# GPS layer, edge loop: edge attributes staged per batch of 28 items by one gather and one store, in place of per round of 56 items by two

## The reference

```
s     = leaky_relu(x_l[src] + x_r[dst] + e_attr @ W_e.T, 0.2)   # 4 heads of 64
alpha = einsum('ehc,hc->eh', s, att)
alpha = softmax of alpha over the edges of one dst
out   = segment_sum(alpha[..., None] * x_l[src], dst)
```

## Time and profile before

| | |
|---|---|
| median of 3 runs | 3459.81 us (3458.88 to 3461.9) |
| span of the profiled execution | 3452.9 us |
| edge loop within it | about 116 to 1530 us |
| PE, DVE, ACT, POOL busy in the whole span | 88%, 53%, 44%, 34% |

### The profile page before, as it was taken

One profiled execution on the slowest core, in us unless ns is written; L12 is line 12 of the kernel. 1 busy time (PEld: TensorE's weight loads), 2 busy tenths in 40 slices (PEclk: granted clock), 3 DMA queues, 4 the chain that ended last, 5 costly groups with the idle time before them and its releaser, 6 DMA issues. The chain is left out here.

```text
span 3452.9 us, 50836 instructions
## 1 busy us (share of the span) xinstructions
PE 3048.3 (88%) x13612; PEld 2420.6 (70%) x13613; DVE 1834.2 (53%) x3643; ACT 1508.7 (44%) x4936; POOL 1189.9 (34%) x1152
## 2 busy tenths in 40 slices
PE   6678888788888888884999999999999999999999
PEld 5456656566565665563778877877787888888898
DVE  5566666666676666676754564374365435111103
ACT  2067666777667676775322322232231212222232
POOL 4556555565555655630310031030021001222210
PEclk9899899999999999997999999999999988999999
DMA  7556655555665655554211011100001032333361
GB/s 217 152 148 148 145 145 141 143 144 141 149 145 145 147 142 150 136 94 124 52 38 37 27 30 31 41 8 1 15 27 50 1 100 84 128 120 119 119 176 38
DMA packets 288628, 345.06 MB, mean 100 GB/s; under 512 B 155176, under 2 KB 213655, under 8 KB 284512
## 3 DMA queue, kind: packets, MB, share of 16 engines
q1 hardware_dynamic: 232813, 174.79, 19.1%
q0 software_dynamic: 53632, 157.89, 17.6%
q10 hardware_dynamic: 2064, 10.81, 1.0%
HBM read 298.03 MB, written 44.37 MB: 99 GB/s over the span
## 5 line engine op out<-in xcount | busy, mean ns | idle before, releaser
L1470 POOL DMA_INDIRECT a_g<-xl_d,a_ix x480 | 468.1, 975 | 311.6 <-issue 116.0
L1504 PE MATMUL b_pM<-b_m,b_oh 128*112 128x281 f32 x1680 | 513.6, 451 | 28.5 <-DVE g_acc L1644 22.5
L1599 ACT ACTIVATE b_m<-a_g,c_pcx 128x64 f32<-128x64 f32 x1856 | 460.4, 334 | 33.6 <-issue 33.6
L1504 PEld LDWEIGHTS b_pM<-b_m,b_oh 128*112 128x112 f32 x1680 | 327.6, 200 | 156.7 <-issue 69.0
L1470 POOL DMA_INDIRECT XS<-xl_d,a_ix x344 | 333.3, 969 | 216.5 <-issue 91.1
L1637 DVE SCALAR_TENSOR_TENSOR a_r<-a_pS,g_attx 128x528 f32<-128x528 f32 x420 | 286.6, 699 | 198.4 <-remote 91.6
L1599 ACT ACTIVATE b_m<-XS,c_pcx 128x64 f32<-128x64 f32 x1424 | 351.5, 333 | 14.3 <-issue 14.2
L2286 ACT ACTIVATE f_hid<-f_pH,f_b 128x256 f32<-128x256 f32 (+3 forms) x360 | 161.9, 451 | 423.0 <-PE f_pH L2180 409.9
L450 PE MATMUL m_pH<-m_h,m_w 128*128 128x313 f32 (+1 forms) x1280 | 342.3, 426 | 4.5 <-DVE m_h L612 4.5
L125 POOL TENSOR_TENSOR m_rstd<-m_ve,m_mhalf 125x5 f32<-125x5 f32 x41 | 48.0, 1170 | 801.5 <-DVE m_ve L111 801.5
L1497 PE MATMUL a_pS<-g_xr,a_lt 128*128 x840 | 237.1, 406 | 97.8 <-ACT a_pS L1581 60.8
(11 more groups left out here) (413 smaller groups left out, 4629.2 us busy)
## 6 DMA issues: line engine op xcount, KB each, us to landing
a_db<-dl_d SPq DMA_DIRECT2D x212, 224.0 KB
f_w<-in_ffn_W1p SPq DMA_DIRECT2D x16, 1024.0 KB
wide_w<-in_ffn_W1p SPq DMA_DIRECT2D x16, 1024.0 KB
m_w<-in_mix_W SPq DMA_DIRECT2D x8, 1024.0 KB
f_w<-in_ffn_W2p SPq DMA_DIRECT2D x8, 1024.0 KB
a_g<-xl_d,a_ix POOLq DMA_INDIRECT x480
a_lt<-eat_d SPq DMA_DIRECT2D x214, 32.0 KB
eat_d<-a_stage SPq DMA_DIRECT2D x15, 448.0 KB
```

Source lines behind the costliest of these rows:

```text
L1470: p.indirect_dma_start(out=gathered(t)[:, j, :], out_offset=None, in_=xl_d, in_offset=bass.IndirectOffsetOnAxis(ap=IX[:, t // BSTEPS, n:n ...
L1504: ins = pe.matmul(pM[0:WN, h, 0:MW], OH[:, b, j, :], M[:, b, j, :], start=(j == 2 * h), stop=(j == 2 * h + 1))
L1599: ins = a.activation(m[:, j, part], gathered(ts)[:, j, part], ACT.Copy, scale=of[:, first + j, h, 0:1])
```

## The change

The input arrays of turned and plain attributes become one array `eab`, whose row for a tile holds 8 KB turned and then 8 KB plain; so do the two scratch arrays. The preparation gathers 128 rows of 16 KB once and stores them once. In the loop the three steps of the staging (tile numbers, gather, store) take place in both batches of a round, at t = 0, 2, 5 and at t = 7, 9, 12, each for 28 items: 28 rows of 16 KB on 28 partitions. A round gathers the same bytes by the same number of gathers (two of 448 KB) and stores them by the same number of stores; it loads tile numbers twice in place of once. The loads of a step read the same runs (512 bytes turned, 64 bytes plain) from rows that are 16 KB apart in place of 8 KB.

```diff
-            eaT = sb("i_eaT", [128, ED * TE])
-            ea = sb("i_ea", [128, ED * TE])
+            eab = sb("i_eab", [128, 2 * ED * TE])
...
-                        a.wait_ge(s["i_ea"], 32)
-                        a.dma_start(eat_d[0:128, :], eaT[:, :]).then_inc(s["i_ea_out"], 16)
-                        a.dma_start(ea_d[0:128, :], ea[:, :]).then_inc(s["i_ea_out"], 16)
+                        a.wait_ge(s["i_ea"], 16)
+                        a.dma_start(eab_d[0:128, :], eab[:, :]).then_inc(s["i_ea_out"], 16)
...
-                        p.indirect_dma_start(out=eaT[:, :], out_offset=None, in_=g["eaT"], in_offset=at).then_inc(s["i_ea"], 16)
-                        p.indirect_dma_start(out=ea[:, :], out_offset=None, in_=g["ea"], in_offset=at).then_inc(s["i_ea"], 16)
+                        p.indirect_dma_start(out=eab[:, :], out_offset=None, in_=g["eab"], in_offset=at).then_inc(s["i_ea"], 16)
...
-                TIX = sb("a_tix", [RI, 1], I32)
-                STG = sb("a_stage", [RI, 2, ED * TE])
+                TIX = sb("a_tix", [BI, 1], I32)
+                STG = sb("a_stage", [BI, 2 * ED * TE])
...
-                        sp.dma_start(LT[WN:128, k, :, :], eat_d[four(base, c), :].rearrange("i (c e) -> c i e", c=ED)).then_inc(s[f"a_eat{k}"], 16)
+                        sp.dma_start(LT[WN:128, k, :, :], eab_d[four(base, c), 0:ED * TE].rearrange("i (c e) -> c i e", c=ED)).then_inc(s[f"a_eat{k}"], 16)
...
-                        if exists(base, t, 0) and t == TILES_AT:
-                            wait(sp, "s_gathered", 32 * i, 0)
-                            sp.dma_start(TIX[:, :], tl_d[staged(i)].unsqueeze(1)).then_inc(s["s_tiles"], 16)
-                        elif exists(base, t, 0) and t == STORE_AT:
-                            sp.wait_ge(s["s_gathered"], 32 * i + 32)
-                            sp.dma_start(eat_d[staged(i), :], STG[:, 0, :]).then_inc(s["s_staged"], 16)
-                            sp.dma_start(ea_d[staged(i), :], STG[:, 1, :]).then_inc(s["s_staged"], 16)
+                        if exists(base, t, 0) and t % BSTEPS == TILES_AT:
+                            wait(sp, "s_gathered", 32 * i, 16 * (t // BSTEPS))
+                            sp.dma_start(TIX[:, :], tl_d[staged(i, t)].unsqueeze(1)).then_inc(s["s_tiles"], 16)
+                        elif exists(base, t, 0) and t % BSTEPS == STORE_AT:
+                            sp.wait_ge(s["s_gathered"], 32 * i + 16 * (t // BSTEPS) + 16)
+                            sp.dma_start(eab_d[staged(i, t), :], STG[:, :]).then_inc(s["s_staged"], 16)
...
-                        if t == GATHER_AT:
-                            p.wait_ge(s["s_tiles"], 16 * i + 16)
-                            wait(p, "s_staged", 32 * i, 0)
+                        if t % BSTEPS == GATHER_AT:
+                            p.wait_ge(s["s_tiles"], 32 * i + 16 * (t // BSTEPS) + 16)
+                            wait(p, "s_staged", 32 * i, 16 * (t // BSTEPS))
                             p.sem_inc(s["a_seen"], 1)
-                            for n, a in enumerate((g["eaT"], g["ea"])):
-                                p.indirect_dma_start(out=STG[:, n, :], out_offset=None, in_=a,
-                                                     in_offset=bass.IndirectOffsetOnAxis(ap=TIX[:, 0:1], axis=0)).then_inc(s["s_gathered"], 16)
+                            p.indirect_dma_start(out=STG[:, :], out_offset=None, in_=g["eab"],
+                                                 in_offset=bass.IndirectOffsetOnAxis(ap=TIX[:, 0:1], axis=0)).then_inc(s["s_gathered"], 16)
```

More of the change, by code:

```diff
@@ L850, in graph_attention @@
 def graph_attention(nc, s, zone, XS, ident, x, xn_d, g, sums_d, scratch, ln1, ln1_of, scale0):
-    key_d, dl_d, eat_d, ea_d, xl_d, wl_d, tl_d, breaks_d, any_d = (scratch[n] for n in ("key", "dl", "eat", "ea", "xl", "wl", "tl", "breaks", "any"))
+    key_d, dl_d, eab_d, xl_d, wl_d, tl_d, breaks_d, any_d = (scratch[n] for n in ("key", "dl", "eab", "xl", "wl", "tl", "breaks", "any"))
     by_head = lambda a: a.rearrange("p (h d) -> p h d", h=GH)
@@ L1015, in _ @@
                     a.activation(DLX[:, n * 128:(n + 1) * 128], pX[(CH + n) % 2], ACT.Copy).then_inc(s["i_dl_out"], 1)
-                a.wait_ge(s["i_ea_out"], 32)
+                a.wait_ge(s["i_ea_out"], 16)
                 a.wait_ge(s["p_xn_d"], 32 * NG)
@@ L1406, in _, with staged @@
                     sp.wait_ge(s["a_const"], 7)
[L1408 to L1410 removed]
+                    def staged(i, t):
+                        at = RI * i + 2 * RI + BI * (t // BSTEPS)
+                        return slice(at, at + BI) if isinstance(at, int) else bass.ds(at, BI)
                     def slot(i, base, t):
[L1413 to L1419 removed]
+                        if exists(base, t, 0) and t % BSTEPS == TILES_AT:
[4 more added lines that the diff above has]
+                            sp.dma_start(eab_d[staged(i, t), :], STG[:, :]).then_inc(s["s_staged"], 16)
                         elif exists(base, t, 0) and t == RING - attributes_ahead:
@@ L1433, in slot @@
                             wait(sp, "b_summed1", base, t - WEIGH - 1)
-                            sp.dma_start(M[:, t % 2, :, EA0:EA0 + ED], ea_d[four(base, t - WEIGH), :].rearrange("i (e c) -> e i c", c=ED)).then_inc(s[f"b_ea{t % 2}"], 16)
+                            sp.dma_start(M[:, t % 2, :, EA0:EA0 + ED], eab_d[four(base, t - WEIGH), ED * TE:].rearrange("i (e c) -> e i c", c=ED)).then_inc(s[f"b_ea{t % 2}"], 16)
                     rounds(sp, slot)
@@ L2501, in gps_layer @@
         scratch = {"key": dram("key_d", (ITEMS * TE + 2,)), "dl": dram("dl_d", (ITEMS, TE)),
-                   "eat": dram("eat_d", (STAGED, ED * TE)), "ea": dram("ea_d", (STAGED, ED * TE)), "tl": dram("tl_d", (STAGED,), I32),
+                   "eab": dram("eab_d", (STAGED, 2 * ED * TE)), "tl": dram("tl_d", (STAGED,), I32),
                    "xl": dram("xl_d", (NW * WN, GD)), "wl": dram("wl_d", (ITEMS,), I32),
@@ L2544, in laid_out @@
     dst = np.pad(a["dst"], (0, spare), constant_values=NOWHERE).reshape(tiles, TE)
-    d = {"x": a["x"].reshape(NT, P, D).transpose(1, 0, 2), "gnn_src": src, "gnn_dst": dst, "gnn_dstT": dst.T, "gnn_ea": ea.reshape(tiles, -1),
-         "gnn_eaT": ea.transpose(0, 2, 1).reshape(tiles, -1)}
+    d = {"x": a["x"].reshape(NT, P, D).transpose(1, 0, 2), "gnn_src": src, "gnn_dst": dst, "gnn_dstT": dst.T,
+         "gnn_eab": np.concatenate([ea.transpose(0, 2, 1).reshape(tiles, -1), ea.reshape(tiles, -1)], 1)}
     d["gnn_W_eT"] = a["L0_gnn_W_e"].T
```

3 lines of the change are left out of this document (removed).

## The result

The changed kernel takes 3482.94 us (median of 4 runs, 3478.51 to 3486.04) against 3460.86 (3458.88 to 3463.84) of the kernel before: a ratio of 1.0059, 95% interval 1.0042 to 1.0076, 22 us more. That is slower by more than the 0.2% that can be told from no change, and inside the range of 3437 to 3491. The likeliest case, no change, is not what happened.

A forecast was written before the change was run, and what follows sets the result against it. Late semaphore releases while POOL issues runs of gathers, 1.46 to 1.48 us per added gather, were taken to bound the loop. Terms summed to 0 to +4 us over 15 rounds: 3459.8 plus about 2 gave 3462 us, range 3437 to 3491.

The forecast's parts named there:

- The likeliest case, no change: Whole kernel: no change that can be told, 3453 to 3467 us, chance 0.37.
- Slower by the clock: Steps at t = 2 and t = 9: PE's lower clock holds after each run of 9; +20 us, 3480, chance 0.25.
- Stage gathers moved, sum 0: POOL's loop: run of 10 becomes 9, -1.5 us; run of 8 at t = 9 becomes 9, +1.5; sum 0.
- One gather of 28 rows of 16 KB takes one place: POOL's stage gathers: each costs one place in a run, 0 extra; bound +3.0 us a round.
- The rival that makes it dearer: POOL's stage gathers: 16 KB rows on 28 partitions take up to two places; up to +45 us, 3505, chance 0.09.
- PE's clock after the run, the middle for both: Steps after both runs of 9: between 7.1 and 8.2 us, so 0 a round, within ±1.1 us.
- Tile numbers, 0 at t = 7: SP's added load at t = 7 arrives before POOL's t = 9: cost 0, or 0.3 us a round if uncovered.
- Regrouping, ± 0.7 us a round with 0 in the middle: POOL's runs in the loop may regroup: one pair of runs of 4 more or less, 10 us in all, either sign.
- Stores, preparation, distance of the rows: 0: Loop stores 0, within ±0.2 us a round; preparation 0, bound -1.3 us once; step reads from rows farther apart 0.
- Faster by the bytes, 0.07: Loop staging: two short bursts hidden where a long one is not; at most -65 us, 3395, half 3428; chance 0.07.

The follow-up runs named there:

- e6_tiles_early: The changed kernel with the next batch's tile numbers loaded at t = 5 and t = 12, before the store: 3443.28 us, ratio 1.0027 to the kernel before.
- e1_split_3: The kernel before with its plain 8 KB-row gather moved to t = 9 and that store to t = 12: 3443.8 us, ratio 1.0027 to the kernel before.
- e3_none_3: The changed kernel without tile numbers, stage gathers and stores in the loop, rereading the first 56 items: 3376.33 us, ratio 0.9821 to the kernel before.
- b_again: The kernel before, unchanged, run again for its profile: span 3458.8 us.
- a_again: The changed kernel, timed and profiled again beside the kernel before: 3473.92 us, ratio 1.0044.
- e5_tiny_apart: The changed kernel without staging, plus unread gathers of 28 rows of 512 bytes at t = 2 and t = 9: 3463.88 us, ratio 0.9994 to the kernel before.
- e7_once_early: The changed kernel with one 56-row gather a round at t = 2, store and next tile numbers at t = 5: 3423.28 us, ratio 0.997 to the kernel before.
- e2_once: The changed kernel with one gather of 56 rows of 16 KB a round at t = 2, stored at t = 5: 3165.08 us, ratio 0.9963 to the kernel before.

## Why it came out so

The time fell into the range, next to the 3480 of *Slower by the clock*, but not for that rival's reason. That it came out inside is luck as far as the mechanism goes: the range was made of clock and regrouping, and the larger part of the loss is a term that the sum did not have.

*Stage gathers moved, sum 0.* Right where POOL starts on time: 13.95 and 14.03 us for the runs of 9.

*One gather of 28 rows of 16 KB takes one place.* Right. It keeps POOL for 898 ns, 19 of the 21 runs of 9 take 13.85 to 14.23 us, the other two, 15.50 and 15.53, end in a late start of POOL, and `e6_tiles_early` with 16 KB rows loses no more than `e1_split_3` with 8 KB. The rival that makes it dearer falls, so far as its sign goes. What the Trainium skill says of ports that partitions reach, weighed in that rival, moved nothing that these runs could tell.

*PE's clock after the run, the middle for both.* Right in kind. PE idled for 3.95 us ahead of the second of the two, where I had 4.5:

```profile
987.75 0.93 PE L1527 MATMUL c_pY<-c_one,c_state 1*116 1x1 f32 x4 [3.95 <-DVE c_state L1716]
```

Behind it the clock was 0.64, and the two stretches together took 15.75 us against 8.2 + 7.1 = 15.3. That is one round. Over the eight regular halves the stretch behind the run of 9 takes 7.39 us, and without the two that follow a late start 7.71; the kernel before has 8.12 and 7.16 in its eight regular rounds, 7.64 on average. So at most 0.1 us a step is left, and the slower clock's rival, which had both at 8.2, is not what happened. The mean clock of the loop did fall, from 0.91 to 0.89, and PE was busy for 19 us more. As PE idles before such a step it may follow from the longer pauses; no run tells the order of the two.

*Tile numbers, 0 at t = 7.* Wrong at its place, and small. I read when SP would issue the load off a round in which a run of 4 came before it. Where a run of 8 does, SP is held back with the others and POOL waits about 5 us, where it pauses 2.9 us at the end of a run of 8 otherwise. Wait by wait that is 8 us too much in the changed kernel (6.73, 5.06 and 5.33 us) and 5 us in the kernel before (5.09 and 5.75), so about 3 us are new. The rows had the sign: 38.0 us in 13 waits are 2.9 us each, not the 1.91 of the one that I read. `e6_tiles_early` took the waits away and lost 10 us, where the full change lost 15 and 22 in other groups. The intervals overlap or nearly touch (1.001 to 1.0043, 1.0028 to 1.0061, 1.0042 to 1.0076), and the changed kernel was never timed beside it in the late regime, so no run confirms the 3 us.

*Regrouping, ± 0.7 us a round with 0 in the middle.* The pattern did break, in over half the loop, and the prediction had said that it would then be wrong. But the break is not what cost the time: regular and irregular halves are equally long, irregular rounds of the kernel before are shorter than its regular ones, and `e3_none_3` is irregular and 57 us faster. The number of POOL's runs went from 146 to 153 between its first stage gather and the start of its last run in the loop, and a run's cost beyond 1.46 us for each gather from 1.05 to 1.15 us (1387.8 us for 846 gathers before, 1414.7 for 848 after; `b_again` and `a_again` have 1.04 and 1.17). 7 × 1.05 + 153 × 0.11 = 24 us is the loss of the loop written in another way, not a cause of it. Seven runs more are 7 us; the larger share is that the average pause got longer.

*What the sum lacked.* It took the pause behind a run as set by the run's length alone. In the changed kernel POOL begins 1.55 us late once in 15 steps, 12 to 17 us of the 24 in the profile of the changed kernel and 15 of 26 in `a_again` by adding them up. No row of the kernel before shows such a start, so the prediction could not have read it there. The late starts stand at the same places in all five profiles of the late regime whose kernels gather 56 staged rows a round (that of the result, `a_again`, `e5_tiny_apart`, `e6_tiles_early`, `e7_once_early`), with rows of 512 bytes as with 16 KB, and in none of the four with 112 rows or no staging. That is what these kernels have in common, not a cause that was tested, and in the other regime the changed kernel has none (`e2_once` has one).

*Stores, preparation, distance of the rows: 0.* The preparation shows nothing: the loop begins within 1.2 us of where it did. For the others nothing speaks against it, and no run took them apart.

*Faster by the bytes, 0.07.* False for the regime in which I predicted, true in the other: there the change gains 13 us and moving a gather alone 20.5. With POOL as the bound, the bytes, stores and tile numbers of before cost about 19 us, and the two kernels that move them in two bursts win back most of that; that the shorter burst is what does it was argued, not taken apart.

What stays open is what makes POOL late once in 15 steps (4.58 us at 1037.49), how the second place costs its 0.27% in `e1_split_3`, and what holds the releases back at all.

## What to carry to other kernels

When engines wait in a fixed rhythm, a sum over the stretches of one good round prices an edit for that round only; compare the mean of all rounds, regular and irregular apart, before you name the loss of the rhythm as the cause. An irregular order beside a longer time is not yet a reason for it. For a pause without a releaser, take the distance from the semaphore's rise to the start: where it jumps from 0.78 to 2.33 us, look at the engine that starts and not at who releases it. Read a load that another engine's step depends on together with what stands ahead of it in its queue, in the worst run-up and not in the usual one. And time a small change in each regime that shows: this one loses 0.4 to 0.6% in one and gains 0.5% in the other.

## What the runs showed of the hardware

The same kernel took 3458 to 3461, 3433, 3175 and 3172 us in different groups of measurements, 8% apart. For the changed kernel, which has a profile in both regimes, 313 of the 321 us between them lie in the loop: in the longer one, engines that wait for semaphores stand still while POOL issues indirect DMAs without a pause (ACT 5.25 us, released "remote", at 1165.17), in the other they don't (between 300 and 1000 us no pause of ACT is longer than 2.85), and POOL's idle time in the loop is 271 us in place of 598. It isn't a chip's number: the second and the last group ran on a chip of the same number, with 3458 and 3172. Whether that was the same piece, and what switches it, these runs don't tell.

An indirect gather's price on POOL barely depends on what it moves: 0.90 us for 28 rows of 16 KB, 0.92 for 56 of 16 KB, 0.91 for 56 of 8 KB, 0.98 for 128 rows, 0.91 for 28 rows of 512 bytes, and 0.30 us to the next.

After a pause POOL begins an indirect gather 0.78 us after the semaphore rose, and in five profiles of the late regime, seven to nine times in each, 2.31 to 2.36 us after it, always at gathers that stand a multiple of 60 apart.
